# Reciprocal roots spread through DRAM instead of TensorE, and scores and values in pairs of steps, in the first attention of a two-part kernel

## The reference, cut to what matters

```
qf, kf = taylor_exp(q), taylor_exp(k)       # 16 heads, 16 features each
A = tril(qf @ kf.T)                         # scores: 1 + s + s^2/2, causal
y = A @ v                                   # 64 values a head
rms = rsqrt(mean(y * y, axis=-1) + eps)     # one number for each token and head
y = y * rms * g_weight
out = y @ Wo.T
```

## Time and profile before

| what | value |
|---|---|
| median of three runs (lowest, highest) | 3383.88 us (3381.18, 3386.66) |
| profiled execution, its own time | 3385.34 us |
| its span, first to last instruction | 3383.5 us |
| busy share PE / DVE / ACT / POOL | 94% / 71% / 76% / 65% |
| mean granted TensorE clock | 0.983 of full speed |
| steps of the first attention | from about 38 to 518 us |
| last sums, roots and output projections | about 519 to 546 us |
| last `AE` ends; first `PJ` of the layers; third `PT` | 518.5; 532.1; 543.8 us |
| first 16 projections of the layers | about 532 to 600 us |
| six layers at their steady pace | about 606 to 3200 us, 56.4 us a period |

### The profile page before, as it was taken

How to read it: one execution, slowest core, us unless ns; L and a number is a source line. 1 busy time by engine, 2 the same in 40 slices (tenths; PEclk the granted TensorE clock), 3 DMA queues, 4 the chain that set the end, 5 groups by cost and what they waited for, 6 DMA issues and landing times.

```text
span 3383.5 us, 125778 instructions
## 1 busy us (share of the span) xinstructions
PE 3179.4 (94%) x52744; PEld 1944.9 (57%) x52744; DVE 2411.4 (71%) x2940; ACT 2557.1 (76%) x5866; POOL 2216.2 (65%) x2135
## 2 busy tenths in 40 slices
PE   7999996899999999999999999999999999999996
PEld 3444442566666666666666666666666666656653
DVE  3656654677777777777777777777777777777773
ACT  5666663687877878887778887878787888788884
POOL 0000003877788777788777887778887778877771
PEclk9999997899999999999999999999999999999998
DMA  3232322444445444554444544444544454544441
GB/s 112 76 81 72 80 71 72 161 157 147 156 154 165 151 152 152 162 162 161 149 152 155 167 157 158 148 155 157 167 153 158 150 162 158 160 149 157 149 141 40
DMA packets 290260, 472.26 MB, mean 140 GB/s; under 512 B 90398, under 2 KB 128540, under 8 KB 289564
## 3 DMA queue, kind: packets, MB, share of 16 engines
q1 hardware_dynamic: 263376, 447.69, 41.6%
q10 hardware_dynamic: 26316, 16.52, 1.7%
HBM read 124.21 MB, written 7.34 MB: 39 GB/s over the span
## 4 chain that ended last, share of the span: by engine, by line
PE 56%; DVE 10%; ACT 8%; SPq 8%; POOL 7%; issue 5%; DMA 5%; POOLq 0%; ACTq 0%; DVEq 0%
PE PS L542 56%; DMA RB<-root_scratch 4%; POOL K L1314 2%; DVE TPB L938 2%; DVE H L990 2%; SPq L528 2%; ACT SC L1227 2%; SPq L499 2%; POOL Q L1332 2%; ACT SX L1203 1%; ACT H L1263 1%; SPq L531 1%; SPq L507 1%; SPq L517 1%; ACT AOT L1240 1%
## 5 line engine op out<-in xcount | busy, mean ns | idle before, releaser
L938 DVE SCALAR_TENSOR_TENSOR TPB<-PS,VEC,C 128x1024 f32<-128x1024 f32 x768 | 970.8, 1275 | 413.4 <-ACT SX L1203 400.6
L1227 ACT ACTIVATE SC<-PS,BQ,RQ 128x64 f32<-128x64 f32 x3072 | 964.0, 431 | 2.8 <-POOL BQ L1350 2.7
L1203 ACT ACTIVATE SX<-PS 128x512 f32<-128x512 f32 x768 | 461.8, 614 | 282.8 <-PE PS L542 282.0
L1314 POOL TENSOR_TENSOR K<-K,RB 128x512 f32<-128x512 f32 x384 | 492.8, 1283 | 153.9 <-DMA RB<-root_scratch 148.3
L1332 POOL TENSOR_TENSOR K<-TPB,TR 128x512 f32<-128x512 f32 x384 | 494.6, 1288 | 0.0
L1332 POOL TENSOR_TENSOR Q<-TPB,TR 128x512 f32<-128x512 f32 x384 | 493.1, 1284 | 0.0
L542 PE MATMUL PS<-LXH,LH 128*128 128x512 f32 x768 | 403.8, 526 | 49.6 <-DVE TPB L938 34.0
L1358 POOL TENSOR_TENSOR SC<-SC,RC 128x1024 f32<-128x1024 f32 x192 | 366.3, 1908 | 29.4 <-DVE RC L961 29.1
L542 PE MATMUL PS<-AOT,LO 128*128 128x512 f32 x768 | 370.0, 605 | 0.0
L542 PEld LDWEIGHTS PS<-PP,VV 64*64 64x64 f32 x12288 | 271.8, 133 | 154.6 <-issue 152.6
L542 PE MATMUL PS<-PP,VV 64*64 64x96 f32 (+1 forms) x12288 | 340.5, 246 | 1.9 <-issue 0.8
(11 more groups left out here) (169 smaller groups left out, 5672.9 us busy)
## 6 DMA issues: line engine op xcount, KB each, us to landing
TR<-TPB SPq DMA_DIRECT2D x768, 256.0 KB, 3.0
RB<-root_scratch SPq DMA_DIRECT2D x768, 128.0 KB, 3.0
PP<-PX SPq DMA_DIRECT2D x1344, 64.0 KB, 2.0
WS<-in_wqkv ACTq DMA_DIRECT2D x72, 128.0 KB, 2.7
PP<-PX SPq DMA_DIRECT2D x192, 48.0 KB, 2.0
QA<-TH SPq DMA_DIRECT2D x128, 64.0 KB, 2.1
QA<-TL SPq DMA_DIRECT2D x128, 64.0 KB, 2.1
KA<-TH SPq DMA_DIRECT2D x128, 64.0 KB, 2.1
```

The costliest lines, as they stand in the source:

```text
L938: e.scalar_tensor_tensor(TPB[:, n % 3:4 + n % 2:3 + n % 2 - n % 3, w, :], g, VEC[:, l, 9 + w:10 + w], C[:, at:at + 1024].rearrange("p (o c ...
L1203: e.activation(SX[i % 3][:, :], bk("PJ", key)[:, :], ACT.Square).then_inc(sem["pj_act"], 1)
L1227: p = e.activation(SC[m % 2][:, g, :, :].rearrange("p x k -> p (x k)"), bank[s][:, at:at + 64], ACT.Exp, bias=BQ[m % 2][:, g:g + 1], scale ...
L1314: e.tensor_tensor(dst, dst, RB[n % 2][:, :], ALU.mult).then_inc(sem["pr_pool"], 1)
```

## The change

- `AI3`, `AM`, `bselr`, `R` and `T[10]` go. A new stage `AT` (SP) writes the roots `T[9]` to DRAM with four DMAs of 8 KB, and `AU` (SP), after they have landed, reads them back with four DMAs of 512 KB, each to 64 partitions, into the new buffer `RX` (8 x 512 numbers on each partition). `AMd` multiplies by `RX`. Its first four pairs of heads wait for the first two DMAs, the rest for the other two.
- `AS`, `ASa`, `ASd` and `AY` are placed in pairs of steps (`t // 2 * 2 + P[st][t % 2]`); there are four probability buffers instead of three.
- Every value in `PLACE` is new, and so the order of many stages, in the layers too. `LS` falls from 221.778 to 216.976.
- The constants load 512 KB less (`bsel`). `VC` waits for the last `AMd`, since its target lies where `RX` was.

```diff
-    "AS": -1.161, "ASa": -1.477, "ASd": -1.154, "AY": 0.847, "AE": 1.944, "AEa": 3.309, "AR": (14.821, 25.002),
-    "AI": (24.677, 25.401, 27.094), "AM": (28.717, 0.812), "AMd": -0.684, "AO": (30.473, 0.702),
+    "AS": (-1.393, -1.358), "ASa": (-1.705, -1.432), "ASd": (-1.460, -1.228), "AY": (1.120, 1.385), "AE": 2.370,
+    "AEa": 3.254, "AR": (14.954, 24.779), "AI": (24.721, 25.518), "AT": 25.806, "AU": 26.064, "AMd": (28.285, 0.350),
+    "AO": (29.648, 0.614), "NM": (36.218, 36.959, 37.194), "AZ": 40.140, "NX": (43.397, 45.136, 45.235), "AW": 48.333,
...
-                at(z + t + P[st], o.put, st, 24 * b + t)
+                at(z + t // 2 * 2 + P[st][t % 2], o.put, st, 24 * b + t)
...
+                elif st == "AT":
+                    b, = key
+                    if b > 1:
+                        for k in range(2):
+                            on.wait_ge(f"rx_in{k}", 32 * b - 32)
+                    on.wait_ge("ai2_dve", 3 * b + 3)
+                    for c in range(4):
+                        e.dma_start(meand[b % 2, 4 * c:4 * c + 4, :], T[9][32 * c:32 * c + 4, :]).then_inc(sem["rt_in"], 16)
+                elif st == "AU":
+                    b, = key
+                    on.wait_ge("rt_in", 64 * b + 64)
+                    if b:
+                        on.wait_ge("am_dve", 8 * b)
+                    for k in range(2):
+                        for s in range(2):
+                            r = meand[b % 2].rearrange("(o c i) x -> o c i x", o=1, c=4)[:, :, 2 * k + s, :]
+                            e.dma_start(RX[64 * s:64 * s + 64, 4 * k:4 * k + 4, :], r.broadcast_to([64, 4, L])).then_inc(sem[f"rx_in{k}"], 16)
...
-                    on.wait_ge("am_pe", no(st, *key))
-                    e.scalar_tensor_tensor(AO[b % 2][:, hp, :], AO[b % 2][:, hp, :], VEC[:, 0, 13:14], bk("AM", key)[:, :], ALU.mult,
+                    on.wait_ge("ae_act", 8 * b + hp + 1)
+                    on.wait_ge(f"rx_in{hp // 4}", 32 * b + 32)
+                    e.scalar_tensor_tensor(AO[b % 2][:, hp, :], AO[b % 2][:, hp, :], VEC[:, 0, 13:14], RX[:, hp, :], ALU.mult,
...
-                    if t > 2:
-                        on.wait_ge("ay_pe", t - 2)
+                    if t > 3:
+                        on.wait_ge("ay_pe", t - 3)
                     on.wait_ge("as_pe", t + 1)
-                    e.activation(P[t % 3][:, :, 0:n], PS[:, 2 * (t % 2):2 * (t % 2) + 2, 0:n], ACT.Square, bias=1.0,
+                    e.activation(P[t % 4][:, :, 0:n], PS[:, 2 * (t % 2):2 * (t % 2) + 2, 0:n], ACT.Square, bias=1.0,
```

More of the change, by code:

```diff
@@ L47 @@
                ("tab", 2048),
-               ("bsel", 1024), ("mask", 512)):
+               ("mask", 512)):
     CONST[_n] = (CONST_COLS, _w)
     CONST_COLS += _w
-KEPT = CONST["bsel"][0]
-STAGED = {n: CONST[n][0] - KEPT for n in ("bsel", "mask")}
+KEPT = CONST["mask"][0]
 def constants():
@@ L185, in order @@
             at(z + P["AR"][n], o.put, "AR", b, n)
-        for i in range(3):
+        for i in range(2):
             at(z + P["AI"][i], o.put, f"AI{i + 1}", b)
+        at(z + P["AT"], o.put, "AT", b)
+        at(z + P["AU"], o.put, "AU", b)
         for t in range(24):
             for st in ("AS", "ASa", "ASd", "AY"):
-                at(z + t + P[st], o.put, st, 24 * b + t)
+                at(z + t // 2 * 2 + P[st][t % 2], o.put, st, 24 * b + t)
         for hp in range(8):
@@ L194, in order @@
             at(z + 3 * hp + P["AEa"], o.put, "AEa", b, hp)
-            t = z + P["AM"][0] + hp * P["AM"][1]
-            at(t, o.put, "AM", b, hp, banks=[(None, "am_dve", 1, 1)])
-            at(t + P["AMd"], o.put, "AMd", b, hp)
+            at(z + P["AMd"][0] + hp * P["AMd"][1], o.put, "AMd", b, hp)
             at(z + P["AO"][0] + hp * P["AO"][1], o.put, "AO", b, hp)
@@ L315, in build @@
         rootd = nc.dram_tensor("root_scratch", (2, 16, L), F32, kind="Internal").ap()
+        meand = nc.dram_tensor("mean_scratch", (2, 16, L), F32, kind="Internal").ap()
         PS = ctx.enter_context(nc.psum_tensor("PS", [128, 8, 512], F32))
@@ L341, in build @@
             KA = sb("KA", [128, 6, L], F32R, ca)
-            sb("gap", [128, 2944], F32, ca)
+            RX = sb("RX", [128, 8, L], F32, ca)
             WOA = sb("WOA", [128, 8, 128], F32, ca)
             AO = [AO0, sb("AO1", [128, 8, L], F32, ca)]
-            bselr = sb("bselr", [128, 1024], F32R, ca)
             XR = [sb(f"XR{i}", [128, L], F32, ca) for i in range(4)]
-            T = [None, None, XIN, XNC] + [sb(f"T{i}", [128, L], F32, ca) for i in range(4, 11)]
+            T = [None, None, XIN, XNC] + [sb(f"T{i}", [128, L], F32, ca) for i in range(4, 10)]
             SQ = [sb(f"sq{i}", [128, L], F32, ca) for i in range(4)]
+            P.append(sb("PA3", [128, 2, L], F32, ca))
             NQ += [sb(f"NQ{i}", [128, L], F32, ca) for i in (1, 2)]
             NZ += [sb(f"NZ{i}", [128, L], F32, ca) for i in (1, 2)]
-            R = [sb(f"R{i}", [128, L], F32R, ca) for i in range(2)]
         LH = sb("LH", [128, 3072], F32R)
@@ L645, in tensor_program @@
                     p.then_inc(sem["ar_pe"], 1)
-                elif st == "AM":
-                    b, hp = key
-                    on.wait_ge("cc_dve", 3)
-                    on.wait_ge("ai3_dve", b + 1)
-                    free(on, st, key)
-                    mm(bk(st, key)[:, :], bselr[:, 128 * hp:128 * hp + 128], R[b % 2][:, :]).then_inc(sem["am_pe"], 1)
                 elif st == "AO":
@@ L826, in vector_program @@
             on.wait_ge("sel_in", 16)
-            for dst, n in ((bselr, "bsel"), (maskb, "mask")):
-                e.tensor_copy(dst[:, :], Vf[0:dst.shape[0], STAGED[n]:STAGED[n] + CONST[n][1]]).then_inc(sem["cc_dve"], 1)
+            e.tensor_copy(maskb[:, :], Vf[:, 0:512]).then_inc(sem["cc_dve"], 1)
             on.wait_ge("c_in", 16)
@@ L895, in vector_program @@
                     root(T[7], T[8], T[9], "ai2", no(st, *key))
-                elif st == "AI3":
-                    two_parts(T[9], T[10], key, st, "ai3")
                 elif st == "AMd":
@@ L1149, in scalar_program @@
                         on.wait_ge("aw_dve", 3)
-                        on.wait_ge("cc_dve", 3)
+                        on.wait_ge("cc_dve", 2)
                     on.wait_ge("av_pe", no(st, *key))
@@ L1170, in scalar_program @@
                     if b:
-                        on.wait_ge("ai3_dve", b)
+                        on.wait_ge("rt_in", 64 * b)
                     on.wait_ge("ai1_dve", b + 1)
                     ln_exp(T[8][:, :], T[7][:, :], T[9][:, :], -0.5, "ai1_act", b + 1)
-                elif st == "AI3":
-                    b, = key
-                    on.wait_ge("ai2_dve", 3 * b + 3)
-                    e.copy(T[10][:, :].bitcast(F32R), T[9][:, :]).then_inc(sem["ai3_act"], 1)
                 elif st == "AO" and key[1] == 7:
@@ L1215, in scalar_program @@
                         on.wait_ge("pv_pe", 8 * u - 4 + 4 * hf)
+                    else:
+                        on.wait_ge("am_dve", 8 * NB)
                     on.wait_ge("vp_pe", j + 1)
```

15 lines of the change are left out of this document (3 added, 12 removed), and 19 rows, old and new, of the table PLACE.

## The result

The kernel after takes 3407.86 us (median of 4 runs, 3403.21 to 3415.03), the kernel before on the same chip 3385.27 us (4 runs). The ratio is 1.0064, with a 95% interval of 1.0043 to 1.0084: slower by 0.6%, where I forecast 3374 us and faster. The time lies in the range (3325 to 3418). The profiled execution of the kernel after took 3403.2 us, the shortest of the four; its span is 3401.4.

The account below looks back on a forecast made before the run. PE was taken to set the time nearly everywhere. 3385.3 + 12 (first attention) - 0.5 (start) - 3 (passage) - 20 (layers) = 3373.8, said as 3374 us; own range 3360 to 3392, wide range 3325 to 3418.

Parts of the forecast that it names:

- The layers: Layers' new order: 12 us less waiting for the feed-forward product, 8 less for K, together 20 us less.
- The pairs: First attention: scores and values in double steps cut 68 runs to 49, saving 3.7 us a batch on PE.
- PE's work: First attention: 60.7 us of PE work a batch falls by 5.7, from double steps (3.7) and AM's removal (2.0).
- five runs of values: First attention: part of the 10.3 us of PE work counted between AR and the first AO.
- the chain that takes the place of TensorE's products: First attention, roots through DRAM: AO can start 15.9 us after AR; PE stands 5.5 us in each of 7 batches.
- The landing: Broadcasts for the first four pairs of heads: 2.6 + 3.3 = 5.9 us, landed 14.9 us after AR.
- upper bound: Wait for AO of 8.6 us if the second DMA lands after 8.3 us, like the 512 KB load at the start.
- The clock: First attention: after each wait PE runs at 0.50 speed for some 4 us, counted as 2.0 us.
- the broadcasts take 8 us: Rival, first attention: 8.6 us of wait and 2.5 for the clock, 12.4 a batch, total 3403 us; chance 0.15.
- The passage: Between first attention and layers: third PT starts at about 23 us instead of 25.3; 3 us less taken.

Follow-up runs that it names:

- e13: Kernel after with the means broadcast for batch 0 only, later batches scaled with them (values not the reference's): 0.9878, 3347.9 us.
- e8: Kernel after with the scratch layout changed so each broadcast reads contiguous 8 KB pieces instead of four of 2 KB: 0.9999, 3388.6 us.
- e14: Kernel before with the roots spread through memory (AT, AU, RX; no AM, AI3, R), single steps and other places kept: 1.0161, 3444.5 us.
- e1: Kernel after with VectorE's copy of the cumulative table (ACd) placed 0.8 units earlier, ahead of AI2: 1.0071, 3411.9 us.
- e17: e13 with the cumulative table's copy (ACd) 0.8 units earlier as in e1: 0.9882, 3347.8 us.
- e12: Kernel after with half the broadcast left out, heads 8 to 15 scaled with the means of heads 0 to 7 (values not the reference's): 1.0002, 3388.4 us.
- e9: Kernel before with only the layers' places of the kernel after, AMd just behind its product in the last batch only: 0.9927, 3362.1 us.
- e6: Kernel before with only the layers' places of the kernel after, AMd just behind its product in every batch: 0.9979, 3381.3 us.

## Why the prediction was wrong

**What was right.** The layers: 20 us less, and from where I said. From the first to the last MX PE is busy for 2602 us before and 2603 after; only its idle time fell, from 109.8 to 89.3 us. What PE waited for from 650 to 3190 us in the kernel after answers to the earlier trace rows:

```profile
PE PS L556 <- DVE H L988: 24.4, 83, 0.7
PE PS L556 <- DVE TPB L936: 23.2, 86, 2.9
...
PE PS L556 <- POOL K L1310: 6.3, 6, 3.3
```

36.8 us for H became 24.4 (12 less forecast, 12.4 found), 16.8 for K became 6.3 (8 less, 10.5 found); the wait for TPB (`PT`), which I had not foreseen, grew by 7. The pairs: a pair of scores takes 0.55 to 0.66 us and a pair of values 1.44 to 1.66 (from 299.76 to 301.42 above), as reckoned from the earlier trace rows. PE's work: 60.7 - 5.7 = 55.0 us a batch was forecast, and with the chain cut (e13) it is busy for 55.4. That this fits so well is in part luck: `AM` was priced at 2.0 us a batch and takes 3.7 from start to next start, and e13's lower clock (0.97 against 0.99) takes some 1 us back. The "five runs of values" between `AR` and `AO` are four; the sum of 10.3 us has the four. The place of the wait, its seven times and the halved clock behind it were as described.

**The step that failed** is the chain that takes the place of TensorE's products. Forecast were 57.0 us busy (55.0 and 2.0 for the clock) and 7.2 idle (1.0, 5.5, 0.3, 0.4) a batch; measured are 59.2 and 8.7. Of the 3.7 us missing, 0.4 is the base (a batch before takes 62.1 us on the mean, not 61.7), 1.8 are the clock's (2.0 against 3.8) and 1.5 are waits; without the base, seven to eight batches make 23 to 26 us of them, about what separates 12 from 38.

- *The landing* was mis-sized: 9.3 us for the first four pairs of heads instead of 5.9. I had divided the bytes by 0.318 MB/us, the mean of the whole kernel when the engines are busy; these DMAs have the engines full at 0.18 to 0.23 MB/us and, in pieces of 2 KB, are at 0.14 in the first 2 us. The nearest row was the one I had called crowded, 8.3 us for 512 KB. Of the 18.3 us from `AR` to `AO` 10.3 were to be work; 6.9 are idle (2.50 and 4.39 above) and the rest is work made slower. So the overrun is 8.0 us, near the 8.6 of the upper bound. e8 shows that the landing decides: with the first scaling 1.6 us sooner behind its DMAs on the mean of eight batches, the batch is 1.5 us shorter, and the whole kernel about 20 us, 5 of them in the passage. At that rate the 3.4 us that I had missed make an estimate of 3 us a batch, stall and clock together, nearly all of the error. By the Trainium skill, page "DMA: Bandwidth & Descriptors" (the table of fixed and variable time), the pair was an estimate of 4.4 us; the page's fit is for DMAs that GpSimd issues, these are SyncE's. The trace does not agree, 9.3.
- *The clock* was mis-sized: a wait was priced at 2.0 us, 4 us of work at 0.50. Behind the waits for `AO` it is 5.3 us of work on the mean of five batches, an estimate of 2.6. The cut gives 3.8 us a batch (e13), the chain alone 5 to 6 (e14). Where the rest falls is open. It isn't simply the bank's wait: behind that the clock fell in two batches of five, with idle times of 1.7 and 2.5 us, and not in the others, with 1.6, 2.5 and 2.5; and such a fall comes with no wait at all in the kernel before, 1.9 us behind sixteen matmuls of 4 and 8 columns, with PE busy all the time:

```profile
285.00:288.50 3.50, 3.50 (x13) 2.42 (x14) 1.88 (x4) 1.24 (x2) 0.00 (x0) 0.51 0.09 25
```

- *The bank of the cumulative product* was overlooked, but it did not lengthen the batch (e1). It and the chain are two waits in the same stretch, and the longer one decides; with both gone the loads of the keys are the third (e17).

The rival "the broadcasts take 8 us" names what happened: its condition, a landing of over 7 us, is met, and 12.4 us a batch for the chain gives 61.7 - 5.7 + 12.4 = 68.4 us (67.9 found) and 3403 us (3403.2 in the profiled execution, 3407.9 at the median). Its single terms fit less well, and that the sum does is partly luck: 8.6 us of wait, where the chain's whole wait is 7.6 (e1), and 2.5 for the clock, where it is 3.8. I gave it 0.15 and set it aside because its row stood in a crowded start; but the broadcasts make such a crowd themselves: two of them, with small loads behind, have the engines at 1.00 to 1.06 from 3 to 7 us after their issue (240 to 244 us in e12).

**The passage** was to be 3 us shorter and was 2 longer. Last values to first MX is 79.7 us before, 81.4 after, 74.2 with the chain cut: the new places are worth 5 us (e9, with the layers' alone, has 76.9), and the last batch's chain takes 7.

**The parts.** Layers alone -24 us (e9), chain alone +55 (e14), all but the chain -41 (e13). Between e9 and e13 lie 17 us for pairs, for `AM`'s removal and the places of the first attention together, where I had 46 for the first two; batch 0 of e13 still has its chain, and the rest is 2.7 us a batch of waits (3.7 idle against 1.0) that the new order has and that the chain hides in the kernel after. That part was too high as well, but nothing of it shows while the chain is there.

## What to carry to other kernels

When work is taken off the bound engine by a detour over other units, reckon the detour from the moment its input is ready to the moment the engine needs it, with the transfer priced by the nearest row of equal size even where that row looks disturbed, and add the slower clock behind each stall. Several waits in one stretch don't add up: take one away and the next stands there, so price a stretch by its longest chain. An order tuned to one dependence has to be found anew for another: moving the products behind the chain cost more than the chain, and one kind of VectorE instruction placed two microseconds later cost some 18 us (e6 against e9).

## What the runs showed of the hardware

- 512 KB broadcasts from DRAM to 64 partitions: of two with nothing large behind them (e12) the last lands after up to 8.9 us, of four after up to 13.1. Four of them and the loads behind keep the DMA engines at 0.8 to 1.1 from 310 to 323 us, at 177 to 252 GB/s.
- About the same bytes (1.67 and 1.63 MB) in 250 packets of mostly 8 KB instead of 836 move at 209 GB/s instead of 140 in the second and third microsecond, the landing falls from 10.0 to 8.3 us, and SP issues four in 2.40 us instead of 3.33.
- 64 KB loads issued right behind them take 6.4 to 8.8 us to land instead of 2.1, though they go between other buffers. Behind two (e12) they take 3.1 to 3.9.
- With idle times of 3.6 to 6.4 us in front, PE's granted clock was at 0.50, the 1.2 GHz level, for 4 to 6 us of work in all five batches looked at; with 1.6 to 2.5 us it fell in two of five, and it also fell with none (kernel before, 285.0 to 288.5 us). With the long wait in every batch the mean over 300 us was 0.91, against 0.97 with it cut (e13) and 0.99 before.
